# A Swin block on one core: the program written out without its engine loop, and three things moved inside a turn

## What is computed

```
y = layernorm(x) * g1 + b1;  y = roll(y, (-3, -3));  windows of 7 x 7 tokens
q, k, v = y @ qkv_w.T + qkv_b                    # 16 heads of 8 channels
attn = softmax(q * 8**-0.5 @ k.T + bias + mask)  # 49 x 49 for each window and head
o = (attn @ v) @ proj_w.T + proj_b;  roll back;  x = x + o
h = layernorm(x) * g2 + b2
out = x + gelu(h @ fc1_w.T + fc1_b) @ fc2_w.T + fc2_b
```

## Time and profile before

| | us |
|---|---|
| median of 3 runs | 4402.23 (4398.28 to 4403.39) |
| the profiled execution's own time | 4409.18 |
| its span in the profile | 4407.4 |

### The profile page before, as it was taken

The page is one execution under the profiler, slowest core; times in us unless marked ns, Lnnn a source line. Parts: engine busy times, 40 slices in busy tenths (PEclk is TensorE's granted clock), DMA queues, the critical chain, the costliest instruction groups (busy, mean ns, idle before and its releaser), DMA issues.

```text
span 4407.4 us, 179808 instructions
## 1 busy us (share of the span) xinstructions
PE 4134.3 (94%) x72586; PEld 3265.2 (74%) x72586; DVE 2743.0 (62%) x6930; ACT 2889.0 (66%) x5120; POOL 2014.4 (46%) x3472
## 2 busy tenths in 40 slices
PE   3999999999999999999999999999999999999998
PEld 2777777777777777777777777777777777777777
DVE  5666665666656656566565656666566566666663
ACT  2666666666666666666666666766666666666665
POOL 4444444444444444444444444444444444444443
PEclk8999999999999999999999999999999999999999
DMA  2333333333333333333333333333333333333332
GB/s 77 102 106 102 98 105 97 105 102 98 105 99 104 109 95 101 98 105 102 99 104 97 105 101 99 105 101 102 94 105 105 99 104 107 104 104 105 106 106 62
DMA packets 626000, 443.34 MB, mean 101 GB/s; under 512 B 158451, under 2 KB 624611, under 8 KB 625059
## 3 DMA queue, kind: packets, MB, share of 16 engines
q1 hardware_dynamic: 624595, 428.82, 32.4%
q0 software_dynamic: 464, 1.81, 0.1%
HBM read 106.07 MB, written 51.46 MB: 36 GB/s over the span
## 4 chain that ended last, share of the span: by engine, by line
PE 82%; ACT 9%; issue 4%; DVE 3%; SPq 1%; DMA 0%; POOL 0%; ACTq 0%; POOLq 0%; DVEq 0%
PE ps L782 18%; PE ps L752 11%; PE ps L766 10%; PE ps L704 10%; PE ps L816 8%; PE ps L739 7%; PE ps L734 7%; PE ps L850 5%; PE ps L796 3%; DVE neg_max L576 2%; ACT L411 2%; ACT v_own L491 2%; PE ps L809 2%; ACT hid L435 2%; ACT probs L418 2%
## 5 line engine op out<-in xcount | busy, mean ns | idle before, releaser
L576 DVE TENSOR_REDUCE neg_max<-ps 113x16 f32<-113x784 f32 x1024 | 998.1, 975 | 514.5 <-PE ps L704 489.4
L418 ACT ACTIVATE probs<-ps 113x784 f32<-113x784 f32 x1024 | 841.1, 822 | 476.1 <-PE ps L739 470.5
L782 PEld LDWEIGHTS ps<-w,hid 128*112 128x112 f32 x7168 | 845.2, 181 | 49.7 <-issue 18.9
L782 PE MATMUL ps<-w,hid 128*112 128x128 f32 x7168 | 865.9, 277 | 0.0
L435 ACT ACTIVATE hid<-ps,col 128x448 f32<-128x448 f32 (+1 forms) x1024 | 541.6, 585 | 420.9 <-PE ps L766 417.8
L739 PE MATMUL ps<-st_q,st_k 128*49 128x196 f16 x8192 | 701.3, 250 | 4.2 <-issue 4.2
L734 PE MATMUL ps<-bias,eye_k 108*64 108x392 f16 x4096 | 686.6, 332 | 0.0
L752 PE MATMUL ps<-probs,v_own 113*32 113x49 f32 x32768 | 584.8, 211 | 101.0 <-issue 71.2
L752 PEld LDWEIGHTS ps<-probs,v_own 113*32 113x32 f32 x32768 | 438.4, 110 | 275.9 <-issue 245.7
L704 PE MATMUL ps<-mx_k,mx_q 128*49 128x196 f16 x8192 | 547.3, 254 | 20.6 <-DMA mx_k<-k_hi 9.3
L739 PEld LDWEIGHTS ps<-st_q,st_k 128*49 128x49 f16 x8192 | 447.0, 105 | 129.2 <-issue 7.1
(11 more groups left out here) (81 smaller groups left out, 6471.9 us busy)
## 6 DMA issues: line engine op xcount, KB each, us to landing
st_k<-k_hi SPq DMA_DIRECT2D x256, 196.0 KB
st_q<-q_hi SPq DMA_DIRECT2D x1024, 49.0 KB
oT_raw<-pv_sb SPq DMA_DIRECT2D x256, 196.0 KB, 2.6
x_in<-in_x SPq DMA_DIRECT2D x224, 196.0 KB
x_res<-in_x SPq DMA_DIRECT2D x224, 196.0 KB
out_y<-y_out SPq DMA_DIRECT2D x224, 196.0 KB
mx_q<-q_hi SPq DMA_DIRECT2D x128, 196.0 KB
mx_k<-k_hi SPq DMA_DIRECT2D x512, 49.0 KB
```

The costliest lines, as they stand in the source:

```text
L418: nc.scalar.activation(probs[0:KP, w % 2, :].rearrange("p (b c) -> p b c", b=2), ps[0:KP, b:b + 2, 0:HB * WT], ACT.Exp).then_inc(s_exp, 1)
L576: nc.vector.tensor_reduce(neg_max[0:KP, :, w, :], ps[0:KP, 0:2, 0:HB * WT].rearrange("p b (h k) -> p b h k", k=WT), AX_X, ALU.max, negate= ...
L782: last = mm(tokens_of(6)[0:TP, i, :], hid[:, c, i * TP:(i + 1) * TP], w_2[:, c, :], start=(c == 0), stop=(c == CH - 1))
```

## The change

Six edits, in five places:

1. `turns` has no loop: all 133 turns are written out on every engine, with constants in place of registers. `apart` is gone; its waits stand on the instructions behind them.
2. PE: fc2 rows 0 and 1 come ahead of the transposes of z1, fc2 rows 2 and 3 ahead of the k and q projections.
3. PE: fc1 pieces 6 and 7 come ahead of v, so that 4 to 7 follow each other.
4. ACT: all eight gelus, then the exponential's table, then the two copies of v.
5. DVE: the reciprocal of the sums comes ahead of the low part of h.
6. DVE: of the two copies of v, the second comes behind x1, between x1 and the first row maximum.

```diff
-        def turns(eng, body):
-            def plain(a, b):
-                for t in range(a, b):
-                    body(t, lambda n: n >= EDGE, lambda k: (t + k) % 2)
-            plain(-2, LOOP_1[0])
-            with eng.Fori(LOOP_1[0], LOOP_1[1] - UNROLL + 1, UNROLL) as t:
-                for later in range(UNROLL):
-                    body(t + later, lambda n: False, lambda k: (LOOP_1[0] + later + k) % 2)
-            plain(LOOP_1[1], STEPS + 3)
+        def turns(body):
+            for t in range(-2, STEPS + 3):
+                body(t, lambda n: n >= EDGE, lambda k: (t + k) % 2)
...
-                        apart(sp, s_r_lo, n)
+                        sp.wait_ge(s_r_lo, n)
...
                 if exists(t - 2):
                     load_table(ACT.Gelu)
-                    for m in range(6):
+                    for m in range(2 * CH):
                         gelu(t - 2, m)
+                if exists(t):
+                    load_table(ACT.Exp)
...
                         nc.scalar.activation(v_place(1, b), v_made(1, b), ACT.Copy).then_inc(s_vown_b, 1)
-                if exists(t - 2):
-                    gelu(t - 2, 6)
-                    gelu(t - 2, 7)
                 if exists(t):
-                    load_table(ACT.Exp)
...
+                n = t - 1
+                if exists(n):
+
+                    dve.wait_ge(s_sum_dma, N_SUM * (n + 1))
+                    nc.vector.reciprocal(sums[:, :, :], sums[:, :, :]).then_inc(s_rsum, 1)
                 n = t - 2
...
-                n = t - 1
-                if exists(n):
-
-                    dve.wait_ge(s_sum_dma, N_SUM * (n + 1))
-                    nc.vector.reciprocal(sums[:, :, :], sums[:, :, :]).then_inc(s_rsum, 1)
...
-                    for b in range(2):
-                        dve.wait_ge(s_v, 2 * n + b + 1)
-                        nc.vector.tensor_copy(v_place(0, b), v_made(0, b)).then_inc(s_vown, 1)
+                    dve.wait_ge(s_v, 2 * n + 1)
+                    nc.vector.tensor_copy(v_place(0, 0), v_made(0, 0)).then_inc(s_vown, 1)
...
                     dve.wait_ge(s_x1, 2 * (n + 1))
+                n = t
+                if exists(n):
+                    dve.wait_ge(s_v, 2 * n + 2)
+                    nc.vector.tensor_copy(v_place(0, 1), v_made(0, 1)).then_inc(s_vown, 1)
...
                     pv(t - 1, NW - 1)
+                if exists(t - 3):
+                    fc2(t - 3, 0, 2)
...
                     max_transposed(t)
-                if exists(t - 3):
-                    fc2(t - 3, 0, 2)
...
                     last.then_inc(s_t2, 1)
+                if exists(t - 3):
+                    fc2(t - 3, 2, 4)
...
-                if exists(t - 3):
-                    fc2(t - 3, 2, 4)
...
                 if exists(t - 2):
-                    fc1(t - 2, 4)
-                    fc1(t - 2, 5)
+                    for m in range(4, 2 * CH):
+                        fc1(t - 2, m)
...
-                if exists(t - 2):
-                    fc1(t - 2, 6)
-                    fc1(t - 2, 7)
```

More of the change, by code:

```diff
@@ L182, in exists @@
         def exists(n):
-            return not isinstance(n, int) or 0 <= n < STEPS
+            return 0 <= n < STEPS
         def past(n, k):
-            return not isinstance(n, int) or n > k
+            return n > k
         def loads(n, edge):
@@ L265, in body @@
                 n = t + 2
-                if exists(n) and not (isinstance(n, int) and n == 0):
+                if exists(n) and n != 0:
                     sp.wait_ge(s_t1, n)
@@ L282, in body @@
                     if past(n, 0):
-                        apart(sp, s_spread, n)
+                        sp.wait_ge(s_spread, n)
                     sp.wait_ge(s_r_lo, n + 1)
@@ L291, in body @@
                     if past(n, 0):
-                        apart(sp, s_rows, NW * n)
+                        sp.wait_ge(s_rows, NW * n)
                     else:
@@ L304, in body @@
                     if past(n, 1):
-                        apart(sp, s_st, NW * (n - 1))
+                        sp.wait_ge(s_st, NW * (n - 1))
                     if past(n, 0):
-                        apart(sp, s_st_dma, N_ST * n)
+                        sp.wait_ge(s_st_dma, N_ST * n)
                     sp.wait_ge(s_lo, 4 * (n + 1))
@@ L323, in body @@
                     if past(n, 0):
-                        apart(sp, s_x1, 2 * n)
+                        sp.wait_ge(s_x1, 2 * n)
                     band_dmas(sp, xr, x_res, n, edge(n), False, s_xres_dma)
-            turns(sp, body)
+            turns(body)
             sp.wait_ge(s_stored, loads(STEPS - 1, True))
@@ L355, in norm @@
                 if past(n, 0):
-                    apart(pool, s_free, n)
+                    pool.wait_ge(s_free, n)
                 for i in range(WS):
@@ L364, in body @@
                 if exists(n):
-                    apart(pool, s_rsum, n + 1)
+                    pool.wait_ge(s_rsum, n + 1)
                     if past(n, 0):
-                        apart(pool, s_rr_dma, N_RR * n)
+                        pool.wait_ge(s_rr_dma, N_RR * n)
                     nc.gpsimd.tensor_scalar(r_hi[:, :, :], sums[:, :, :], 1.0, 0.0,
@@ L373, in body @@
                                             ALU.subtract).then_inc(s_r_rest, 1)
-                    apart(pool, s_r_rest, n + 1)
+                    pool.wait_ge(s_r_rest, n + 1)
                     nc.gpsimd.tensor_scalar(r_lo[:, :, :], sums[:, :, :], LOW_SCALE, 0.0,
                                             ALU.mult, ALU.add).then_inc(s_r_lo, 1)
-                    if isinstance(n, int) and n == 0:
+                    if n == 0:
                         pool.wait_ge(s_w, 16 * N_W)
@@ L396, in body @@
                     norm(n, s_ln2, mv2, ve2, s_ve2, rs2, s_rs2, mr2, s_mr2, nm2, s_nm2, x1, z2, s_t2, s_z2)
-            turns(pool, body)
+            turns(body)
         @block.scalar
@@ L500, in body @@
                             copy_pv(t, w - 1)
-            turns(act, body)
+            turns(body)
         @block.vector
@@ L519, in aggregate @@
             def aggregate(n, st, s_st_, mv, s_mv):
-                apart(dve, s_st_, n + 1)
+                dve.wait_ge(s_st_, n + 1)
                 for i in range(WS):
@@ L566, in finish @@
                     if past(n, 0):
-                        dve.wait_ge(s_stored, loads(n - 1, edge(n) and (not isinstance(n, int) or edge(n - 1))))
+                        dve.wait_ge(s_stored, loads(n - 1, edge(n) and edge(n - 1)))
                 dve.wait_ge(s_fc2, 2 * n + p + 1)
@@ L668, in body @@
                             aggregate(n, st2, s_st2, mv2, s_ln2)
-            turns(dve, body)
+            turns(body)
         @block.tensor
@@ L869, in body @@
                         max_logits(t + 1, w, edge)
-            turns(pe, body)
+            turns(body)
 def kernel(**inputs):
```

11 lines of the change are left out of this document (2 added, 9 removed).

## The result

| | before | after |
|---|---|---|
| median of the runs, us | 4402.81 | 4227.84 |
| profiled execution's own time, us | 4409.18 | 4228.27 |
| its span, us | 4407.4 | 4226.5 |

The ratio is 0.9606, with a 95% interval of 0.959 to 0.9623: 175 us less, where 183 were forecast (4219). The time lies in the range and near the forecast. The terms do not fit as well: the loop gave less than its term and the moves more, as the experiments show.

What follows compares the result with a forecast made beforehand. PE's own sequence with its few pauses was taken to set a turn's length; 4409.2 - 144.6 (loop) - 39 (edits 2 to 6) = 4225.6 us profiled, 4219 as median after 7.0 off; range 4188 to 4266.

Steps and rivals of the forecast that it cites:

- its term: Loop, turns 4 to 107: written out, they take 3373.8 us and not 3518.4, a gain of 144.6 us.
- the moves: Edits 2 to 6, turns 3 to 127: gain 0.64 - 0.33 = 0.31 us each, 39 us in all.
- I take -145, since 19 turns in a row show it: Loop: of the bounds -108 and -145 us, takes the larger gain, from late written-out turns at 32.44 us each.
- the jump's price: PE at each of 12 jumps back: 6.5 us pause plus half-clock work, 9 us a jump, 108 in all.
- the step that all small pauses go with the loop: PE in the loop: small pauses vanish with the jumps when written out, making the gain 145 us and not 108.
- the 7 off the sum: Whole kernel: sum of 4225.6 us against the profiled execution, lowered by 7.0 because the runs' median is lower: 4219.
- only the jumps go: Loop on PE: the small pauses stay, so the gain is 108 us and not 145, time 4256; chance 0.13.
- 0.15 us by the like wait: DVE, second v copy: waits 0.15 us for x1 on its own engine, part of the 0.33 us a turn cost.
- the chain over DVE: DVE and PE, eight windows: row maximum, next `max_logits`, next row maximum wait for each other; delay of 0.33 us stays.
- The sum: Whole kernel: 4409.2 - 144.6 - 39 = 4225.6 us against the profiled execution, 4219 us as median.

Runs made afterwards that it cites:

- the first two experiments: Kernel before with its loop written out, old order and separate wait instructions kept: 4288.13 us; the same with plain waits without the increment: 4285.45 us.

## Why the prediction was right, and which terms were off

- **What bounds the kernel.** Right: PE's own sequence with its pauses. Busy 95% before, 99% after in the same window.
- **Edit 1.** The mechanism was right, the size was not. The step "I take -145, since 19 turns in a row show it" took the price of all 104 turns from the last ones. The 104 turns went from 3518.40 to 3394.18 us with the loop alone written out, 124 less: 20 us of small pauses stay in the middle turns, 0.19 a turn. Of the 145 the turns around jumps held 103 and the other turns of the loop 41, so the jump's price was right and the step that all small pauses go with the loop was wrong. The medians differ by 114. Four of the remaining ten are outside those turns (the span fell by 120.2). The rest is that the profiled execution of before was 7 us above its median while this one is 1 above: the prediction took its term from that slower execution and the 7 off the sum besides, as if an execution after would stand as far above its median (it stood 0.4 above).
- **The rival "only the jumps go".** By the ratios it was the nearer one for this term: 108 forecast, 114 measured. Its reason was half right, since some of the small pauses were not the loop's at all.
- **Edit 2.** 0.64 a turn forecast, 0.61 by undoing it (0.59 between turns without a pause). fc1 was at 8.15 where 8.10 was worked out. Its price was right, and so was the reason: the row maximum was over when the z1 transposes came.
- **Edits 3 to 5.** Counted at nothing, measured -4 (edits 3 and 4) and +3 us (edit 5) when undone, with no pause of PE's on q's low part or on r_rows in the changed kernel. The traces show a loss of 0.07 a turn up to the logits that the prediction did not have; the earlier exponential brings `pv` 0.10 ahead, and the copy of v in front of the row maximum hides that, as the prediction said it would be hidden.
- **Edit 6.** Right in sign and place (the first row maximum right behind the copy, `max_logits` waiting for it), wrong in size: 0.33 forecast, 0.18 between turns without a pause, 16 us by undoing it and not 41. (The 0.10 between logits and second `max_logits` in the trace after is this 0.18 less the 0.07 or 0.08 that the earlier exponential gave.) The second `max_logits` was worked out at 2.91 behind the logits and came at 2.68. The largest part of the 0.23 is "0.15 us by the like wait": that wait was an instruction of its own, and the one in the changed kernel took 0.03. The rest is smaller: the row maximum started 0.14 ahead of the copy's end in place of 0.08, it lasted 0.93 in place of 0.97, and 0.05 and not 0.08 lay behind it. The prediction also took the chain over DVE for what set the old start. The second `max_logits` before started at 4000.21, when the 0.49 of `pv` from 3999.72 were over and 0.14 behind the row maximum, so it was `pv` that held it.
- **The sum** came out 9 us low because two larger errors partly offset each other: the moves brought 58 and not 39, the loop with `apart` 116 and not 145. That the total came so near is partly luck; only undoing the terms one by one showed that.

## What to carry to other kernels

A jump back in a long unrolled loop cost some 8 us here, so the gain from writing it out goes with the number of jumps; take the price of a written-out turn from all parts of the program, not from its quietest stretch. Where an engine waits at a turn's start for another engine's last item, look for independent work that is already due, and put it there: that one move brought the whole gain of the moves. Work that another engine's idle time covers costs nothing until it is put between two links of the chain, as the copy of v was.

## What the runs showed of the hardware

- At a jump, PE stood 6.2 us on the mean in a body of 8 turns and 5.1 in one of 4. Behind the one shown it then had half its clock for some 8 us. In all, a jump made the two turns around it 7.7 to 8.6 us longer, by the three bodies of 4, 8 and 26 turns.
- DVE started 0.15 us after its own result when the wait was an instruction of its own with an increment, and 0.04 when the wait stood on the instruction itself (the first two experiments).
- Loading and storing 7 rows as 4 and 3, with twice the DMA issues and the same bytes, took 10 us of PE's pauses away in 104 turns, though PE waited for none of those transfers there.
